# Reordering TensorE and ScalarE inside five attention sublayers, and moving one normalisation to GpSimd

## What is computed

```python
x = _layernorm(x + _L1_attn_ref(x, ...))                 # "diff":   differential, rope, no mask
x = _layernorm(x + _L1_xattn_ref(x, ctx_1024, ...))      # "causal": keys and values from the context
x = _layernorm(x + _L2_attn_ref(x, ...))                 # "alibi":  additive bias
x = _layernorm(x + _L2_xattn_ref(x, ctx_1024, mask...))  # "keys":   key mask, no output projection
x = _layernorm(x + _L3_xattn_ref(x, ctx_1024, mask...))  # "full":   full mask

# all five, by sequence and head:
scores = einsum('bihd,bjhd->bhij', qh, kh) * scale (+ mask or bias)
attn = einsum('bhij,bjhd->bihd', softmax(scores), vh);  out = attn @ W_o + b_o

# differential only: 8 pairs of heads share a value of width 16
diff = probs[:, :, 0] - lam * probs[:, :, 1]
attn = einsum('bhts,bhsd->bhtd', diff, v)
attn = attn * rsqrt(mean(attn * attn, axis=-1) + 1e-05) * (1.0 - LAMBDA_INIT)
```

## Time and profile before

| | us |
|---|---|
| median of 3 runs (lowest, highest) | 4104.81 (4103.65, 4107.08) |
| the profiled execution: its time | 4081.88 |
| the profiled execution: its span | 4080.1 |
| TensorE busy | 3018.0 (74%) |
| VectorE busy | 2256.7 (55%) |
| GpSimd busy | 1789.2 (44%) |
| ScalarE busy | 1718.3 (42%) |
| first scores of diff, causal, alibi, keys, full start at | 938.6, 1429.8, 2173.3, 2514.6, 3406.2 |
| last scores of diff, causal, alibi, keys, full start at | 1372.0, 1729.1, 2472.2, 2814.5, 3705.8 |

### The profile page before, as it was taken

One profiled execution on the slowest core, in us unless ns is written; L12 is line 12 of the kernel. 1 busy time (PEld: TensorE's weight loads), 2 busy tenths in 40 slices (PEclk: granted clock), 3 DMA queues, 4 the chain that ended last, 5 costly groups with the idle time before them and its releaser, 6 DMA issues. The chain is left out here.

```text
span 4080.1 us, 81328 instructions
## 1 busy us (share of the span) xinstructions
PE 3018.0 (74%) x27802; PEld 2047.6 (50%) x27802; DVE 2256.7 (55%) x6213; ACT 1718.3 (42%) x3334; POOL 1789.2 (44%) x1575
## 2 busy tenths in 40 slices
PE   3399907767777599946747996886899867997693
PEld 2387805554455356634524664554344434666572
DVE  2002336536777577751235775886777576775123
ACT  0144404334444366602214664664555554662341
POOL 2544272225565455523344554664022354552534
PEclk9999959888998799955558998998898788997896
DMA  6377611020010112114521112221000001221573
GB/s 215 115 227 218 191 41 45 6 7 24 32 41 31 53 55 73 55 41 122 136 76 41 55 53 67 76 86 59 1 1 1 1 3 47 77 67 56 160 224 106
DMA packets 305037, 304.44 MB, mean 75 GB/s; under 512 B 91108, under 2 KB 226821, under 8 KB 304648
## 3 DMA queue, kind: packets, MB, share of 16 engines
q1 hardware_dynamic: 269160, 252.01, 20.1%
q0 software_dynamic: 16384, 33.59, 2.8%
q10 hardware_dynamic: 19232, 15.50, 1.2%
HBM read 161.27 MB, written 55.84 MB: 53 GB/s over the span
## 5 line engine op out<-in xcount | busy, mean ns | idle before, releaser
L802 DVE TENSOR_TENSOR moe_first_tile_y<-moe_first_out_ps,moe_first_expert_w 128x256 f32<-128x256 f32 x78 | 33.1, 425 | 336.5 <-PE moe_first_out_ps L937 336.4
L998 POOL DMA_INDIRECT slot_x<-x_tok,moe_first_slots x128 | 123.7, 967 | 177.8 <-DVE moe_first_slots L775 75.1
L978 ACT ACTIVATE moe_first_hid<-moe_first_hid_ps,moe_first_expert_w 128x256 f32<-128x256 f32 x312 | 128.2, 471 | 155.6 <-PE moe_first_hid_ps L926 155.6
L1012 POOL DMA_INDIRECT moe_first_token_y<-slot_y,moe_first_slots x128 | 123.8, 967 | 100.4 <-issue 65.2
L1665 POOL TENSOR_TENSOR causal_k_blocks<-causal_k_T,headmask 128x1024 f32<-128x1024 f32 x64 | 121.2, 1896 | 105.9 <-PE causal_scores L1277 101.9
L2783 PE MATMUL L_ffn_experts<-L_ffn_expert_w,x_T 128*128 128x512 f32 x256 | 166.2, 735 | 1.8 <-ACT L_ffn_expert_out L2880 1.8
L1665 POOL TENSOR_TENSOR alibi_k_blocks<-alibi_k_T,headmask 128x1024 f32<-128x1024 f32 x64 | 121.2, 1896 | 105.2 <-PE alibi_scores L1277 101.2
L1665 POOL TENSOR_TENSOR full_k_blocks<-full_k_T,headmask 128x1024 f32<-128x1024 f32 x64 | 121.2, 1896 | 93.8 <-PE full_scores L1277 89.5
L937 PE MATMUL moe_first_out_ps<-moe_first_expert_w,moe_first_hid 128*128 128x128 f32 x1248 | 162.2, 281 | 0.0
L1416 ACT ACTIVATE diff_probs_T<-diff_pT 128x512 f32<-128x512 f32 x128 | 76.4, 597 | 183.0 <-PE diff_pT L1291 183.0
L1665 POOL TENSOR_TENSOR keys_k_blocks<-keys_k_T,headmask 128x1024 f32<-128x1024 f32 x64 | 120.7, 1896 | 74.7 <-PE keys_scores L1277 71.1
(11 more groups left out here) (544 smaller groups left out, 9152.3 us busy)
## 6 DMA issues: line engine op xcount, KB each, us to landing
moe_first_expert_w<-in_L_attn_experts SPq DMA_DIRECT2D x78, 578.0 KB, 4.0
moe_last_expert_w<-in_L_ffn_experts SPq DMA_DIRECT2D x46, 578.0 KB, 4.1
slot_x<-blank ACTq DMA_DIRECT2D x2, 4992.0 KB, 44.2
moe_first_tile_x<-slot_x SPq DMA_DIRECT2D x78, 128.0 KB, 4.1
slot_y<-moe_first_tile_y SPq DMA_DIRECT2D x78, 128.0 KB, 1.9
L_ffn_tile_x<-slot_x SPq DMA_DIRECT2D x64, 128.0 KB, 2.3
slot_y<-L_ffn_tile_y SPq DMA_DIRECT2D x64, 128.0 KB, 1.8
moe_last_tile_x<-slot_x SPq DMA_DIRECT2D x46, 128.0 KB, 3.9
```

The lines of the kernel that those rows point to most:

```text
L802: dve.tensor_tensor(y_out[:, q, :, :], out_bank[q][:, 0:SLOT_TILE].rearrange("p (s d) -> p s d", s=SPAN), over(wall[:, j % RING, 2 * FF + ...
L978: act.activation(hid[:, j % 2, b, :], hid_bank[b // 2][:, SLOT_TILE * (b % 2):SLOT_TILE * (b % 2) + SLOT_TILE], gelu, bias=wall[:, j % RIN ...
L998: pool.indirect_dma_start(slot_x[part][:, :], bass.IndirectOffsetOnAxis(slots[:, part, r, t:t + 1], 0), net.x_tok[:, part * K + t, :], Non ...
L1012: pool.indirect_dma_start(y_in[:, p, k, r, :], None, slot_y[part][0:NT * SLOT_TILE, :], bass.IndirectOffsetOnAxis(slots[:, part, r, t:t + ...
```

## The change

Three edits. First, on TensorE `mix_values(t-1)` moves from ahead of `turn(t, 0)` to between `turn(t, 0)` and `turn(t, 1)`. Second, on ScalarE the exponentials of one half each stand behind a copy: `copy_turned(t, 0)`, `exponentials(t+1, 0)`, the extra, `copy_turned(t, 1)`, `exponentials(t+1, 1)`. Third, in diff alone, the two value projections move from k = 1 and 2 to k = 2 and 3, with their copies on ScalarE, and the multiplication of `rms_output` moves from VectorE to GpSimd, straight behind the power. `V_AT` is 2 in all five: that is where the value projection already stood in the other four.

```diff
+    V_AT = PER - VP if lambdas is not None else PER - 1 - VP
...
                     if n:
                         pe.wait_ge(v_copied, nth(c, 2 * VP, 2 * n))
-                    if wo is not None and c.shift(-2 - late).inside(CHUNKS) and n == VP - 1:
+                    if wo is not None and c.shift(-2 - late).inside(CHUNKS) and n == 0:
                         pe.wait_ge(oT_copied, done(c.shift(-2 - late)))
...
                         if rope:
                             pe.wait_ge(rope_mult, done(c.shift(2 + late), 4))
-                            pe.wait_ge(v_copied, nth(c.shift(2 + late), 2 * VP, 2))
...
                             scores(t.shift(1))
+                        turn(t, 0)
                         if t.shift(-1).inside():
                             mix_values(t.shift(-1))
-                        turn(t, 0)
...
                         turn(t, 1)
-                        if PER - 1 - VP <= k < PER - 1 and c.shift(1).inside(CHUNKS):
-                            project_values(c.shift(1), k - (PER - 1 - VP))
+                        if 0 <= k - V_AT < VP and c.shift(1).inside(CHUNKS):
+                            project_values(c.shift(1), k - V_AT)
...
                         copy_turned(t, 0)
+                        if t.shift(1).inside():
+                            exponentials(t.shift(1), 0)
...
                         copy_turned(t, 1)
                         if t.shift(1).inside():
-                            exponentials(t.shift(1))
-                        if PER - 1 - VP <= k < PER - 1 and c.shift(1).inside(CHUNKS):
-                            copy_values(c.shift(1), k - (PER - 1 - VP))
+                            exponentials(t.shift(1), 1)
+                        if 0 <= k - V_AT < VP and c.shift(1).inside(CHUNKS):
+                            copy_values(c.shift(1), k - V_AT)
...
-                        if k == 0 and diff and c.shift(-2).inside(CHUNKS):
-                            rms_output(c.shift(-2))
...
                     pool.tensor_tensor(rms_inv[:, :], ms_eps[:, :], minus_half[:, :], ALU.pow).then_inc(rms_done, 1)
+                    pool.wait_ge(rms_done, done(c))
+                    hold(pool)
+                    if c.shift(-2).exists:
+                        pool.wait_ge(oT_ready, done(c.shift(-2)))
+                        hold(pool)
+                    pool.tensor_tensor(o_heads[:, c.u % 2, :, :].rearrange("p t (k d) -> p (t k) d", k=8),
+                                       o_diff[:, c.u % 2, :, :].rearrange("p t (k d) -> p (t k) d", k=8),
+                                       spread_last(rms_inv[:, :], dv), ALU.mult).then_inc(o_normed, 1)
```

22 lines of the change are left out of this document (6 added, 16 removed).

## The result

| | before | after |
|---|---|---|
| median (lowest to highest), 4 runs each | 4105.92 (4103.65 to 4107.08) | 4037.78 (4034.76 to 4042.68) |
| ratio, 95% interval | | 0.9833 (0.9817 to 0.9849) |
| profiled execution: time, span | 4081.88, 4080.1 | 4035.01, 4033.3 |

68 us were saved, where 147 were forecast. The direction was right and the size was not: 4037.8 lies above the range's upper end of 4012.

What follows compares the result with a forecast made beforehand. TensorE's order was taken to bound causal, alibi and full; TensorE and VectorE, nearly level, keys; a chain of waits diff. Savings of 67 + 31 + 49 = 147 us took 4104.8 to 3957.8, rounded 3958; range 3925 to 4012.

Steps and rivals of the forecast that it cites:

- the idle time ahead of second transposes: TensorE waiting for a bank ScalarE empties; in causal 0.99 and 0.64 us, 1.63 per chunk, all predicted to vanish.
- the rope's wait: In diff, TensorE's 4.20 us wait for rope products ahead of the first value projection; its removal was to gain 2.7 per chunk.
- the wait of 1.5 ahead of `turn_rows`: In diff, a new TensorE wait of about 1.5 us for ScalarE's copies of the second value projection.
- part 1: Mixing between the transposes on TensorE: 1.5 us saved per chunk in causal, alibi and full, 2.1 in keys.
- the step from transposes to the mixing: TensorE's gap between a transpose and the mixing behind it, taken as zero, between -0.1 and +0.1 us a tile.
- The 0.64: In causal at k = 2, TensorE's idle us left between the two transposes despite `turn_output`, expected to vanish.
- ties: In causal, near-equal arrivals of TensorE's work and what it needs from VectorE or ScalarE; allowed 0.15 us per chunk altogether.
- Rival B: Outside diff, half the gain is lost to TensorE waiting for exponential, copy or division: 98 us saved, time 4007; chance 0.13.
- the 17.05 us of VectorE's work: In keys, VectorE's chunk once 2.45 us of waits are saved, the expected new bound; 17.4 with ties.
- Part 2: Exponentials between ScalarE's copies, to have probabilities ready for the earlier transpose; costed at nothing, cover 0.4 us.
- 2.7 - 3.0: In diff, values later: 2.7 us per chunk gained at the rope wait, 3.0 lost to VectorE idling behind `turn_rows`.
- 3.44: In diff, us per chunk VectorE saves when the head normalisation moves to GpSimd: 2.17 of work plus 1.27 of waiting.

## Why the prediction was right and wrong

**Right.** The sublayers' paces before, and the idle time ahead of second transposes: it vanished at k = 1 and 2. In diff the rope's wait, the wait of 1.5 ahead of `turn_rows` (1.58) and the 3.0 us of VectorE behind it (3.14) came as worked out; the multiplication was cheaper on GpSimd (1.06 against 1.26) and hidden.

**Wrong, part 1, the step from transposes to the mixing.** "I take zero for it, between -0.1 and +0.1 a tile." It is 0.17 in 61 of 64 tiles, 0.68 us a chunk. I had read the step from mixing to transposes and taken the other direction for alike, while a row of the same trace had the like one, a value projection 0.17 behind its transposes (1540.07).

**Wrong, part 1, what is late next at k = 2.** The 0.64 there was counted as gained. The same copies on ScalarE that held the second transposes also held the value projection right behind them; it had never shown, because the transposes waited in front of it. With that wait gone it came up, 0.44 a chunk. Both terms are 1.12 us against the 0.15 allowed for ties. The chunk saves 0.64 where I had 1.5; 1.5 - (1.12 - 0.15) = 0.53, so 0.1 saved beyond that is unaccounted for. The price of the first term is read from rows; no run takes it away. Rival B, with half of the gain lost to small waits of TensorE, described the three sublayers in size, but named the wrong waits: neither exponential nor division was late.

**Wrong, keys.** 31 us forecast, -5.9 measured. The step that failed is the 17.05 us of VectorE's work: it was taken from a trace in which most of its long operations happened to fall clear of GpSimd's. Shortening TensorE's chunk moved them onto it, and by the means 4 x 0.647 + 0.765 = 3.4 us a chunk came on top, on the engine that I had named as the next bound: 17.05 + 3.4 = 20.4, against 20.46 measured. The forecast of the freed pace was right within 0.4: with the mask out of the way a chunk takes about 17.0 (262.3 against 300.1 is 2.5 less than 19.5). Its bound was not: at 260.5 of 262.0 us busy that is TensorE, not VectorE.

The Trainium skill has the rule ("SBUF — State Buffer", section "SBUF: two separate sides"): VectorE and GpSimd share one pair of SBUF ports; a VectorE operation in a two-port mode and a GpSimd operation exclude each other for a whole instruction, and so does a VectorE operation with two SBUF inputs against one of GpSimd that reads SBUF. The rows agree in the main: `o_diff` and the residual in keys, with two SBUF inputs, and the normalisation go to two to about five times their length, and operations that read PSUM stay as they are. Whether the normalisation, with one SBUF tensor as input, runs in such a mode no row shows; that it is stretched, 335 to 1204 ns, they do. I had cited a rule of this kind for the one multiplication that moved, and there it cost nothing that shows. It had to be asked of every VectorE operation whose time in the chunk would shift. The description of the core above, by which the engines meet only at semaphores, is too narrow for these rows.

**Part 2, costed at nothing.** Behind the first edit the exponentials' order gives 3 to 4 us a sublayer, and alone it costs 6 to 11. The forecast took the two as one and could not see it; its reason for the second, an exponential in time for the earlier transpose, was right, and its price of nothing was not.

**Diff, terms of the sum.** Two runs split the gain: 433.4 to 422.5 by the values later, to 409.2 by the first two edits on top, to 396.0 by the move to GpSimd; by chunk, over 15, 0.73, 0.89 and 0.88, each uncertain by some 0.3. I had forecast -0.3 (2.7 - 3.0), nothing, and 3.44. The term that failed most is the last: a busy time and a wait taken off VectorE were counted in full as time off the chunk, "VectorE loses 2.17 of work and the 1.27 it waited for the power". VectorE did lose them (3.87), but now waits 2.3 a chunk for scores, where it would wait 0.2 with the heads still on it, and its operations beside GpSimd's spreading grew by 2.5 us a chunk, a cost that was nowhere in the sum. That growth comes with the values moved later, whichever engine multiplies: with the values later alone `o_diff` takes 700 ns and the normalisation 590 in the mean, against 393 and 340. There it accounts for what the edit was worth: idle time for scores falls from 3.91 to 10.5/11 = 0.95 a chunk, 2.96 less, the two operations take 4 x 0.307 + 4 x 0.25 = 2.2 more, and 0.7 is left, as measured. The steady chunk saved 2.8, near the 3.15 of the sum, by errors that offset each other, which is luck; over the whole sublayer, with its lighter first and last chunks, 37.4 came of 49.

**Diff, a term left out: the clock.** The earlier trace rows has 0.90 for diff, and the sum never priced it. Along the split above the clock over diff reads 0.91, 0.90, 0.93 and 0.95. So the first step owes nothing to it, while of the other two, 13.3 and 13.2 us, up to 14 and 9 can be clock by the estimate above. No run holds the clock fixed, so how much is shorter waits and how much is the same work at a higher clock stays open.
